# Two-layer graph kernel on one core: chunk 0's first pieces in half the rows, chunk 1's first halves by two blocks, the last means taken off on ACT

## The reference

```python
sim  = tanh(adj * adj)                    # 350 largest of a row are kept
h2   = tanh(x @ W_proj + b_proj)
feat = relu(sim @ (h2 @ W_gcn) + b_gcn)   # layer 0
x1   = layernorm(x + feat)
pos, neg = (adj > 0) @ x1, (adj < 0) @ x1
edge = adj @ x1                           # layer 1
y    = concat(pos, neg) @ node_w + node_b * diag(adj) + edge @ edge_w + edge_b * diag(adj)
out  = layernorm(x1 + y)
```

## Time and profile before

| | us |
|---|---|
| median of 3 runs | 610.4 (609.98 to 610.6) |
| the profiled execution's own time | 611.33 |
| its span | 609.5 |
| PE busy in the span | 600.4 (99%) |
| DVE, ACT, POOL busy | 473.8, 420.3, 187.7 |
| mean granted clock of TensorE | 0.999 of full speed |

### The profile page before, as it was taken

One profiled execution on the slowest core, in us unless ns is written; L12 is line 12 of the kernel. 1 busy time (PEld: TensorE's weight loads), 2 busy tenths in 40 slices (PEclk: granted clock), 3 DMA queues, 4 the chain that ended last, 5 costly groups with the idle time before them and its releaser, 6 DMA issues.

```text
span 609.5 us, 5805 instructions
## 1 busy us (share of the span) xinstructions
PE 600.4 (99%) x1972; PEld 342.0 (56%) x1972; DVE 473.8 (78%) x690; ACT 420.3 (69%) x315; POOL 187.7 (31%) x88
## 2 busy tenths in 40 slices
PE   9998999999999999999999999999999999999996
PEld 6643444444444444555655655655655656557995
DVE  3867978888887979986697696796797786886743
ACT  3787686868768686558884883983893883875960
POOL 0587798887979697000000000000000000000000
PEclk9999999999999999999999999999999999999999
DMA  8999999999999990048789388486495685784000
GB/s 239 342 341 348 332 323 322 306 276 324 276 329 278 330 205 1 10 129 253 221 234 271 95 251 226 132 239 197 139 270 159 173 240 155 213 231 126 2 17 20
DMA packets 139455, 130.67 MB, mean 214 GB/s; under 512 B 9763, under 2 KB 139430, under 8 KB 139430
## 3 DMA queue, kind: packets, MB, share of 16 engines
q1 hardware_dynamic: 74390, 66.22, 39.4%
q10 hardware_dynamic: 65040, 64.17, 36.5%
HBM read 128.27 MB, written 2.10 MB: 214 GB/s over the span
## 4 chain that ended last, share of the span: by engine, by line
PE 90%; DMA 5%; DVE 2%; SPq 1%; POOL 1%; ACT 1%; issue 0%; DVEq 0%; ACTq 0%
PE acc L1059 34%; PE acc L1045 32%; PE stage L1068 10%; PE stage L1067 10%; DMA a_rows<-in_adj_dram 5%; PE stage L1059 2%; PE to_rows L1074 1%; PE to_rows L1073 1%; DVE a_cols L673 1%; SPq L401 1%; PE to_rows L1024 1%; POOL a_cols L390 0%; DVE a_cols L662 0%; ACT a_cols L593 0%; DVE rhs L685 0%; POOL a_cols L384 0%
## 5 line engine op out<-in xcount | busy, mean ns | idle before, releaser
L662 DVE STREAM_TRANSPOSE a_cols<-a_rows 128x2048 f32<-128x2048 f32 x120 | 278.1, 2325 | 81.3 <-PE stage L1068 51.9
L1045 PE MATMUL acc<-a_cols,rhs 128*128 128x512 f32 x512 | 221.7, 593 | 2.4 <-ACT a_cols L593 1.8
L1059 PE MATMUL acc<-a_cols,x_rows 128*128 128x512 f32 (+1 forms) x512 | 216.2, 565 | 0.0
L1045 PEld LDWEIGHTS acc<-a_cols,rhs 128*128 128x128 f32 x512 | 96.5, 190 | 121.9 <-issue 117.1
L390 POOL TENSOR_TENSOR a_cols<-a_cols 128x1536 f32<-128x1536 f32 x56 | 153.2, 2746 | 35.3 <-DVE a_cols L662 34.9
L1059 PEld LDWEIGHTS acc<-a_cols,x_rows 128*128 128x128 f32 x512 | 96.0, 189 | 86.3 <-issue 81.0
L593 ACT ACTIVATE a_cols<-a_cols 128x2048 f32<-128x2048 f32 x56 | 107.1, 1913 | 49.9 <-POOL a_cols L390 49.3
L611 ACT ACTIVATE a_rows<-a_rows 128x4096 f32<-128x4096 f32 x32 | 116.0, 3624 | 26.1 <-DVE a_cols L662 13.0
L1067 PE MATMUL stage<-masks,x_hi 128*128 128x512 f32 (+1 forms) x288 | 126.7, 448 | 0.0
L614 ACT ACTIVATE a_rows<-a_rows 128x4096 f32<-128x4096 f32 x32 | 116.0, 3624 | 1.0
L1068 PE MATMUL stage<-masks,x_lo 128*128 128x512 f32 (+1 forms) x288 | 103.1, 367 | 0.0
(11 more groups left out here) (119 smaller groups left out, 277.5 us busy)
## 6 DMA issues: line engine op xcount, KB each, us to landing
a_rows<-in_adj_dram ACTq DMA_DIRECT2D x120, 512.0 KB, 9.8
a_rows<-in_adj_dram SPq DMA_DIRECT2D x120, 512.0 KB, 9.5
out_dram<-n_rows SPq DMA_DIRECT2D x28, 64.0 KB, 7.4
x_rows<-in_x_dram ACTq DMA_DIRECT2D x8, 64.0 KB, 2.3
x_rows<-in_x_dram SPq DMA_DIRECT2D x8, 64.0 KB, 2.1
x_rows<-in_x_dram ACTq DMA_DIRECT2D x4, 128.0 KB, 3.5
x_rows<-in_x_dram SPq DMA_DIRECT2D x4, 128.0 KB, 4.3
diag<-in_adj_dram SPq DMA_DIRECT2D x32, 0.5 KB
```

The lines of the kernel that those rows point to most:

```text
L662: nc.vector.transpose(half_out(hs), half_in(s, h % HALVES)).then_inc(turned[layer], 1)
L1045: last = nc.tensor.matmul(acc[parity][:], rhs[:, b, :], a_cols[:, h % HSLOTS, k, :], start=(b == 0), stop=(b == BLOCKS - 1))
L1059: last = nc.tensor.matmul(sums, x_rows[:, b, :], rows(a_cols[:, h % HSLOTS, k, :]), start=(b == 0), stop=(b == BLOCKS - 1))
```

## The change

Three things change.

**Chunk 0.** The first two pieces (h = 0 to 3) are loaded in two halves of the rows: 256 KB loads, first those with the first 256 rows of all four quarters (their own semaphore `rows_loaded`), then the others. They are turned, squared, put through tanh and multiplied in units of 256 rows by 4 blocks, in the order (0,0) (1,0) (0,1) (1,1), where the first number is the half and the second the part of the rows. The halves 4 to 7 keep their pairs of blocks. ACT issues the eight small loads in the head, two ahead of it and one after each of the first six `hid` steps; all its later loads of layer 0 move back by one half.

**Chunk 1.** The halves 8 to 11 go by pairs of blocks, as in chunk 0; 12 to 15 stay whole. PE's loop over chunks starts two chunks later, and the first two bodies are written out.

**The end.** In the second part of the last chunk, DVE negates the means, ACT adds them to the sums (two ACTIVATE with a bias, into `n_rows`), and DVE multiplies both tiles by the reciprocal root in one `tensor_tensor`.

```diff
+    BY_ROWS = 2
+    UNITS = [(s * HALVES + e, k) for s in range(BY_ROWS) for k in range(2) for e in range(HALVES)]
+    BY_BLOCKS = HPC + 2 * HALVES
+    UNITS += [(h, k) for h in range(BY_ROWS * HALVES, BY_BLOCKS) for k in range(2)]
-    EARLY = [("rhs", 5), ("rhs", 6)]
+    EARLY = {("rhs", 5): 2, ("rhs", 6): 2}
...
+        def unit(t, h, k):
+            cols = t[:, h % HSLOTS, :, :]
+            if h < BY_ROWS * HALVES:
+                return cols[:, :, k * CH // 2:(k + 1) * CH // 2]
+            return cols[:, k * PAIR:(k + 1) * PAIR, :].rearrange("p b c -> p (b c)")
...
+        def first_rows(s, q, k):
+            at = slice(k * ROWSETS // 2, (k + 1) * ROWSETS // 2)
+            return quarter_of(s, q)[:, at, :], quarter_in((0, 0), s, q)[:, at, :]
...
+            for s in range(BY_ROWS):
+                for q in SP_QUARTERS:
+                    sp.dma_start(*first_rows(s, q, 0)).then_inc(rows_loaded[s], 16)
+                for q in SP_QUARTERS:
+                    sp.dma_start(*first_rows(s, q, 1)).then_inc(a_loaded[s], 16)
...
-                    if g >= ACT_FIRST:
-                        load_ahead(len(ACT_QUARTERS) + g - ACT_FIRST)
+                    if g < FIRST_LOADS - 2:
+                        load_first(g + 2)
+                    else:
+                        load_ahead(BY_ROWS * len(ACT_QUARTERS) + g - (FIRST_LOADS - 2))
...
-            HEAD_LOADS = len(ACT_QUARTERS) + GROUPS - ACT_FIRST
+            HEAD_LOADS = BY_ROWS * len(ACT_QUARTERS) + GROUPS - (FIRST_LOADS - 2)
...
+                for h, k in units_of(c):
+                    if before and (h % HPC, k) == (2, 0):
+                        act.wait_ge(b_gcn_loaded, 16)
+                        relu_out(before)
+                    first_unit(h, k)
+                    if k == 1:
+                        load_ahead(HEAD_LOADS + h)
...
+            act.wait_ge(mean_negated, 1)
+            for k in range(tiles):
+                ins = nc.scalar.activation(n_rows[:, LAST[2], at + k, :], last_rows[1][k], ACT.Identity,
+                                           bias=minus_mean[:, k:k + 1])
+            ins.then_inc(centred, 1)
...
+                    if root_of:
+                        nc.vector.tensor_scalar(minus_mean[:, 0:tiles], mean_var[:, 0:tiles, 0], -1.0, None, ALU.mult)\
+                            .then_inc(mean_negated, 1)
...
+                        waited(centred, 1)
+                        nc.vector.tensor_tensor(rows, rows, r.unsqueeze(2).broadcast_to([P, tiles, F]), ALU.mult)\
+                            .then_inc(normed, 1)
...
+                        by_rows = h < BY_ROWS * HALVES
+                        rows = slice(k * CH // 2, (k + 1) * CH // 2) if by_rows else slice(0, CH)
+                        for b in range(HB) if by_rows else range(k * PAIR, (k + 1) * PAIR):
+                            at = block_of(h % HPC, b)
+                            last = nc.tensor.matmul(acc[parity][:, rows], rhs[:, at, :],
+                                                    a_cols[:, h % HSLOTS, b, rows], start=(h % HPC == k == b == 0),
+                                                    stop=(at == BLOCKS - 1))
...
-            chunks(pe, layer0)
+            chunks(pe, layer0, 1)
```

More of the change, by code:

```diff
@@ L240, in build @@
         wl1_loaded = sem("wl1_loaded")
+        rows_loaded = [sem(f"rows_loaded{k}") for k in range(BY_ROWS)]
         a_loaded = [sem(f"a_loaded{k}") for k in range(SLOTS)]
@@ L298, in build, with chunks @@
         g_stored = sem("g_stored")
-        def chunks(eng, body):
+        def chunks(eng, body, apart=0):
             body((0, 0, 0), None)
-            with eng.Fori(0, (CHUNKS - 2) // 2) as pair:
+            for pair in range(apart):
+                body((pair * 2 + 1, pair, 1), (pair * 2, pair, 0))
+                body((pair * 2 + 2, pair + 1, 0), (pair * 2 + 1, pair, 1))
+            with eng.Fori(apart, (CHUNKS - 2) // 2) as pair:
                 body((pair * 2 + 1, pair, 1), (pair * 2, pair, 0))
@@ L318, in next_of, with units_of, whole_halves @@
             return c + 1, span + parity, 1 - parity
+        def units_of(c):
+            return [(h, k) for h, k in UNITS if h // HPC == c]
+        def whole_halves(c):
+            return range(max(c * HPC, BY_BLOCKS), (c + 1) * HPC)
         def is_first(c):
@@ L379, in layer0 @@
             def layer0(chunk, before):
[L380 to L384, removed]
+                for h, k in units_of(chunk[0]):
+                    part = unit_squared(h, k)[0]
+                    if k == 0:
+                        pool.wait_ge(unit_in_cols, h + 1)
+                        nc.gpsimd.tensor_tensor(part, part, part, ALU.mult).then_inc(unit_squared_pool, 1)
+                    else:
                         pool.wait_ge(turned[0], h + 1)
-                        nc.gpsimd.tensor_tensor(second, second, second, ALU.mult).then_inc(squared_pool, 1)
-                        continue
+                        nc.gpsimd.tensor_tensor(part, part, part, ALU.mult).then_inc(squared_pool, 1)
+                for h in whole_halves(chunk[0]):
                     part = flat(a_cols, h % HSLOTS)[:, 0:SQ_POOL]
-                    pool.wait_ge(turned[0], chunk[0] * HPC + h + 1)
+                    pool.wait_ge(turned[0], h + 1)
                     nc.gpsimd.tensor_tensor(part, part, part, ALU.mult).then_inc(squared_pool, 1)
@@ L524, in load_ahead, with first_unit @@
                     load_quarter(rows_of(0, (c, c // 2, c % 2)), s, ACT_QUARTERS[q])
[L526 to L540, removed]
+            def first_unit(h, k):
+                cols, rest = unit(a_cols, h, k), unit_squared(h, k)[1]
+                if k == 0:
+                    act.wait_ge(unit_in_cols, h + 1)
+                    nc.scalar.activation(rest, rest, ACT.Square).then_inc(unit_squared_act, 1)
+                    act.wait_ge(unit_squared_act, h + 1)
+                    act.wait_ge(unit_squared_pool, h + 1)
+                    nc.scalar.activation(cols, cols, ACT.Tanh).then_inc(unit_tanh, 1)
+                else:
+                    act.wait_ge(turned[0], h + 1)
+                    nc.scalar.activation(rest, rest, ACT.Square).then_inc(squared_act, 1)
+                    act.wait_ge(squared_act, h + 1)
+                    act.wait_ge(squared_pool, h + 1)
+                    nc.scalar.activation(cols, cols, ACT.Tanh).then_inc(tanh_done, 1)
             def square_rest(n):
@@ L678, in _ @@
                     continue
-                if (kind, g) in EARLY:
-                    turn_pairs(EARLY.index((kind, g)))
+                for _ in range(EARLY.get((kind, g), 0)):
+                    turn_unit(*next(early))
                 dve.wait_ge(staged, n + 1)
@@ L763, in layer0 @@
             def layer0(chunk, before):
-                if not before:
-                    for h in range(len(EARLY), HPC):
-                        turn_pairs(h)
-                    return
-                for h in range(HPC):
-                    turn(0, chunk[0], h)
-                    if h in (4, 5, 6):
-                        norm0(before, h - 4)
+                for h, k in units_of(chunk[0])[0 if before else sum(EARLY.values()):]:
+                    turn_unit(h, k)
+                for h in whole_halves(chunk[0]):
+                    turn(0, chunk[0], h % HPC)
+                    if h % HPC in (4, 5, 6):
+                        norm0(before, h % HPC - 4)
             each_chunk(layer0)
```

105 lines of the change are left out of this document (63 added, 42 removed).

## The result

The changed kernel takes 612.04 us in the median of 22 runs (610.24 to 614.42), against 610.47 in 22 runs of the kernel before on the same chip (609.68 to 611.68): a ratio of 1.0023, 95% interval 1.0015 to 1.0031. It is slower, by 1.6 us, and outside the range of 608.5 to 611.5. The profiled execution took 613.46 us, with a span of 611.6. It lies 1.4 us above the median of the runs (before's lies 0.8 to 0.9 above its own), so what the profile shows as lost is more than in the usual run.

The account below looks back on a forecast made before the run. PE, busy 99% of the span, was taken as the bound, with the landing at 58.08 holding chunk 2's start equally. Terms 0 + 0 + 0.3 us took 610.4 to 610.1 us, range 608.5 to 611.5.

Parts of the forecast that it names:

- Chunk 0's units: Start of chunk 0: first turns end 1.1 us sooner, so PE starts at 23.10, 0.6 us earlier.
- Chunk 1's pairs and the relu: Chunk 1: the 1.76 us gap goes, start 2.3 us earlier; the relu holds PE's turns to 54.9, leaving 1.8.
- the 1.8 us are given back: Chunk 2's start: PE arrives at 79.5 but waits 1.8 us for half 16's tanh at 81.34; start parts sum to 0.
- the prediction's last sentence: Forecast is wrong if the landing at 58 moves over half a microsecond or chunk 2 starts other than at 81.4.
- The chain behind the landing: From half 12's landing at 58.08 through DVE, POOL and ACT to half 16's tanh at 81.34: 23.26 us, without PE.
- Loads moved back ... I take 0: ACT's loads from chunk 1 on, one half (3.43 us) later: 10.5 us ahead against median landing 10.9, lateness hidden; 0.
- ACT's loads come late, in every chunk: Rival, chance 0.07: late ACT loads delay DVE at each chunk's half 4; PE loses 0.5 a chunk, time 613.1.
- The end: Last chunk's second part: means taken off on ACT and one multiply bring the output 0.3 us earlier, at 606.61.
- All of this is on the path: At the end: the whole 0.3 us by which the output comes earlier was counted as time saved.
- a rival of its own: Small loads move slower, chance 0.11: landing at 58.08 comes 2.2 us later, time 612.3; the skill's fit gave near 618.

Follow-up runs that it names:

- the kernel with one load more ahead: The changed kernel with all of ACT's layer 0 loads one place earlier, the later ones back where they stood before the change: 610.45 us, ratio 0.9998.
- the run with chunk 1's pairs alone: The changed kernel with chunk 0 and all loads (512 KB) as before, chunk 1's pairs and the new end kept: 610.47 us, ratio 1.0003.
- later loads alone: The kernel before with one load fewer issued by ACT in the head, so its later layer 0 loads go out one half later: 613.53 us, ratio 1.0044.

## Why the prediction was wrong

**Chunk 0's units**: right. PE starts with no idle time ahead of it (22.88 against 23.72).

**Chunk 1's pairs and the relu**: right in kind. The gap is gone; PE turns at 53.86, 1.0 us before the 54.9 forecast. PE reached that point 0.4 us before the 54.3 worked out, and the relu did not hold it, because the piece landed at 44.88 and not at 46.00 and the relu's chain with it. With the landing at 45.42, in the kernel with one load more ahead, PE does wait 0.17 us for the relu.

**Chunk 2's start, "the 1.8 us are given back"**: the mechanism is right, and the run with chunk 1's pairs alone shows it with 81.52. In the changed kernel the landing itself came at 56.89 and not at 58.1, so chunk 2 starts 1.1 us early (80.25), and the sum was off by that; the prediction's last sentence had named a landing moved by over half a microsecond as a sign of being wrong. The chain behind the landing had its length right: 23.3 worked out, and 23.36, 23.34, 23.41 and 23.35 us from the landing to chunk 2's start in the four kernels with pairs in chunk 1 and whole halves behind them. What moved the landing is open, and the 1.1 us count as luck. DVE started half 12 at 58.08, 58.23, 58.17, 57.33 and 56.78 in the five kernels with loads of 512 KB, and at 56.89, 57.45, 57.12, 56.73 and 57.36 in the five with small ones. The means differ by 0.6 us, and one kind alone spreads over 1.45. The two at 58.17 and 56.78 issue the same loads in the same order up to that point, so one execution can differ from another by 1.4 us there.

**"Loads moved back ... I take 0"**: this is the step that failed. The rival "ACT's loads come late, in every chunk" took place, with 3.1 us lost in the profile where its example had 3, though not by 0.5 us a chunk but mostly in the last three. I had worked out the 10.5 us that the load has, and set against it the median landing of 10.9, with 0.9 us of slack at PE. The slack was right (0.8 measured). Three things were wrong. First, the median was taken where the load of each chunk has its own time: 11.55, 10.5, 11.6, 11.2 and 12.2 us in the five chunks, all within the 9.3 to 12.9 that was on the table, and three of them more than the 11.4 that lead and slack cover together. Second, the lead was taken as fixed. ACT issues that load 10.2 us ahead of PE's turns in the first of these chunks and 9.4 to 9.6 us ahead in the following ones, so that the 10.5 us became 9.7 to 9.8. Third, "a queue with one load less in it is shorter" does not hold: ACT's loads take 11.0 us in the median as against 10.9, and SP's 13.0 as against 11.0. A turn that comes late makes ACT's tanh behind it late, and with it the next load; that this is what shortens the lead is argued, not shown. With 10.5 and 0.9 of slack against a spread of 9.3 to 12.9, a chance of 0.07 was far too small.

**The end**: the output came 0.3 us earlier, to the hundredth as worked out (1.89 against 2.20), and alone it brought the span's end forward by 0.3. "All of this is on the path" did not hold in the changed kernel, where one of ACT's stores was issued slowly and the span ended no earlier. It was a small term.

So the sum should have read: 1.2 earlier at chunk 2, 3.1 later up to layer 1, 0.2 later at the end, together 2.1 later in the span (611.6 against 609.5), and 1.6 in the median of the runs. The Trainium skill's advice in "DMA: Bandwidth & Descriptors", section Bandwidth, Measured, against small loads had been a rival of its own (the 2 us of fixed cost, which the prediction named with it, the page gives in another section, Anatomy of one DMA, for loads that GpSimd issues; here SP and ACT issue them). The trace shows no loss from the size in this stage: 14 to 20 us moved 348 GB/s with the 256 KB loads under way (330 in the earlier trace rows), and 345 to 349 in all five kernels with small loads. Windows of the changed kernel, with the columns of the earlier trace rows:

```profile
14.00:20.00 6.00, 6.00 (x39) 4.70 (x38) 3.01 (x5) 3.69 (x6) 0.28 (x1) 1.00 1.10 348
20.00:34.00 14.00, 14.00 (x77) 12.48 (x76) 11.67 (x12) 12.04 (x19) 12.13 (x9) 1.00 1.10 345
```

## What to carry to other kernels

When an edit moves where a load is issued, compare the time that it then has, and the slack behind it, with the upper end of the landing times of the loads of that queue, and not with the median: here one place later in ACT's program cost 3 us by itself, more than the change had won. Look at the landings that a wait ends with; the longest of a view can be those of loads that nobody waits for. When a gap closes and the gain is given back at the next landing, the cure is to shorten the chain behind that landing (pairs of blocks for the halves 12 to 17 gave 1.3 to 1.5 us), not to feed PE earlier ahead of it. And look at what is queued behind an instruction that is added at the end: stores too.

## What the runs showed of the hardware that was not expected

Issuing ACT's loads one step later left their own landing times as they were and lengthened those of SP's: from a median of 11.0 us to 13.0 in the changed kernel and 12.7 in the one with later loads alone, the longest from 12.9 to 16.3 and 16.8 (12.9 to 14.0 in the eight kernels in which DVE waits for none of them after half 12). Why is open. The time at which DVE starts half 12, right behind the landing, moves by 1.4 us between two executions that issue the same 512 KB loads in the same order (56.78 and 58.17), more than most terms of such a sum. Issuing a 32 KB store on ACT took 0.34 to 0.48 us, but in three kernels one of the four took 0.69 to 1.32.
